# Values turned by VectorE and DRAM, position tables as one stationary square, and q two items ahead

## The reference, cut to what matters

```python
qkv = hidden_states @ qkv_w + qkv_b                      # 16 heads of 64
q, k, v = (qkv[0], qkv[1], qkv[2])
attn = jnp.einsum('bqc,bkc->bqk', q * scale, k)
rel_h = jnp.einsum('bhwc,hkc->bhwk', rq, Rh)             # rq: q by rows and columns
rel_w = jnp.einsum('bhwc,wkc->bhwk', rq, Rw)             # Rh[h, k] = rel_pos_h[h - k + 15]
attn = attn + rel_h[:, :, :, :, None] + rel_w[:, :, :, None, :]
attn = jax.nn.softmax(attn.reshape(B * nH, H * W, H * W), axis=-1)
out = attn @ v
return out @ proj_w + proj_b
```

## Time and profile before

| | us |
|---|---|
| median of 3 runs | 1245.13 (1244.61 to 1247.14) |
| the execution profiled | 1246.36 |
| its span | 1244.4 |
| TensorE busy | 1216.4 |
| VectorE / ScalarE / GpSimd busy | 690.4 / 475.1 / 641.5 |
| TensorE's mean granted clock, share of 2.4 GHz | 0.997 |

### The profile page before, as it was taken

The page is one execution under the profiler, slowest core; times in us unless marked ns, Lnnn a source line. Parts: engine busy times, 40 slices in busy tenths (PEclk is TensorE's granted clock), DMA queues, the critical chain, the costliest instruction groups (busy, mean ns, idle before and its releaser), DMA issues.

```text
span 1244.4 us, 19555 instructions
## 1 busy us (share of the span) xinstructions
PE 1216.4 (98%) x6768; PEld 975.0 (78%) x6768; DVE 690.4 (55%) x1434; ACT 475.1 (38%) x1229; POOL 641.5 (52%) x726
## 2 busy tenths in 40 slices
PE   6999999999999999999999999999999999889998
PEld 4788896478888888888888878777887787668887
DVE  7534444775665433666452578756347776476212
ACT  3611141034645320656341164644206555243212
POOL 4633389256565567555546655555665556464000
PEclk9999999999999999999999999999999999999999
DMA  5211124025564643454645356557535565620012
GB/s 185 84 46 48 34 56 117 8 65 160 154 169 137 184 134 97 127 177 128 185 136 166 86 160 212 180 160 223 168 102 151 175 209 156 205 60 1 29 40 68
DMA packets 129376, 155.03 MB, mean 125 GB/s; under 512 B 30080, under 2 KB 84000, under 8 KB 129280
## 3 DMA queue, kind: packets, MB, share of 16 engines
q1 hardware_dynamic: 118976, 146.92, 39.7%
q10 hardware_dynamic: 10304, 6.88, 1.8%
HBM read 111.81 MB, written 37.75 MB: 120 GB/s over the span
## 4 chain that ended last, share of the span: by engine, by line
PE 89%; DVE 5%; ACT 2%; issue 1%; DMA 1%; SPq 1%; POOL 0%; ACTq 0%; DVEq 0%; POOLq 0%
PE PS L1137 53%; PE PS L682 7%; PE PS L1758 7%; PE PS L1183 4%; PE PS L960 3%; PE PS L969 2%; PE PS L975 2%; PE PS L1227 2%; PE PS L1216 2%; PE PS L1775 2%; PE PS L1247 2%; PE PS L665 1%; PE PS L1197 1%; DVE bst L257 1%; PE PS L700 1%
## 5 line engine op out<-in xcount | busy, mean ns | idle before, releaser
L1137 PE MATMUL PS<-XB,w_hi 128*128 128x512 f32 x1024 | 340.5, 397 | 1.2 <-POOL w_lo L228 1.2
L226 POOL CAST w_hi<-w_raw 128x512 fp32r<-128x512 f32 x195 | 124.2, 637 | 307.5 <-PE PS L1137 213.0
L228 POOL TENSOR_TENSOR w_lo<-w_raw,w_hi 128x512 fp32r<-128x512 f32 x195 | 256.1, 1313 | 15.6
L1137 PEld LDWEIGHTS PS<-XB,w_hi 128*128 128x128 f32 x1024 | 192.2, 188 | 47.1 <-issue 5.0
L1137 PE MATMUL PS<-XB,w_lo 128*128 128x512 f32 x512 | 200.2, 391 | 0.0
L1137 PE MATMUL PS<-XB,part 128*128 128x512 f32 x768 | 190.3, 394 | 0.0
L1137 PEld LDWEIGHTS PS<-XB,part 128*128 128x128 f32 x768 | 141.9, 188 | 32.2 <-issue 2.3
L1373 ACT ACTIVATE part<-PS,nmax 128x256 f32<-128x256 f32 (+1 forms) x256 | 112.2, 443 | 141.6 <-DVE nmax L1485 93.2
L1383 ACT ACTIVATE part<-part,prec 128x256 f32<-128x256 f32 (+1 forms) x256 | 105.8, 476 | 27.7 <-DVE prec L1500 27.7
L228 POOL TENSOR_TENSOR part<-part,part 128x512 fp32r<-128x512 f32 x85 | 111.5, 1312 | 6.8
L1137 PE MATMUL PS<-part,w_hi 128*128 128x512 f32 x344 | 112.9, 395 | 1.5 <-DVE part L1544 1.5
(11 more groups left out here) (136 smaller groups left out, 1884.0 us busy)
## 6 DMA issues: line engine op xcount, KB each, us to landing
w_raw<-in_w SPq DMA_DIRECT2D x187, 256.0 KB, 2.8
part<-in_w SPq DMA_DIRECT2D x85, 256.0 KB, 2.8
turned<-part SPq DMA_DIRECT2D x128, 128.0 KB, 2.9
part<-turned SPq DMA_DIRECT2D x32, 512.0 KB, 5.0
turned<-part SPq DMA_DIRECT2D x128, 96.0 KB, 2.5
part<-turned SPq DMA_DIRECT2D x32, 384.0 KB, 4.0
strips<-part ACTq DMA_DIRECT2D x16, 256.0 KB, 2.7
out_x<-xT SPq DMA_DIRECT2D x16, 256.0 KB, 2.1
```

The costliest lines, as they stand in the source:

```text
L226: pool.tensor_copy(hi, raw).then_inc(w_hi_done, 1)
L228: pool.tensor_tensor(lo, raw, hi.bitcast(F32), ALU.subtract).then_inc(w_ready, 1)
L1137: m = nc.tensor.matmul(PS[:, bank, :], wt[:, (c % 4) * P:(c % 4) * P + P], rhs(hl, c), start=c == k == 0, stop=c == CK - 1 and k == 2)
```

## The change

- Values: V's product is turned in 32 × 32 blocks by DVE straight from PSUM (`turn_values`), written to DRAM by four DMAs, read back by one, and put in order by ACT (`take_v`). TensorE's four transposes go. The values' bias is added later, to the heads' result (the probabilities of a row sum to one).
- Position products: both tables and both heads form one stationary square of 128 × 128, q is the moving operand of 512 columns: 3 matmuls an item for 24. DVE turns the result (`turn_relative`), four DMAs write it.
- Order: Q's product of i+2 stands right behind K's of i+1. relative(i+2) stands in V's product of i after five chunks; attend(i−1) behind V's product (with j = 0 ahead of it). On ACT and DVE evac_q(i+2) and rest_of_q(i+2) stand near the end of item i, behind the normalization; evac_o(i−2) and rest_of_o(i−2) come first.
- Probabilities of all four head and image parts lie in one buffer and go to DRAM in four DMAs an item instead of eight.
- End: six PSUM banks for the last output product instead of three, its first halves spread over both last attends, and another placing of `build_m`.

The diff, cut to its core:

```diff
+            if i + 2 < ITEMS:
+                take_block(i + 2, "Q")
             take_block(i, "V", range(0 if i else 1, 2))
             if s and j == 0:
                 for o in range(CK):
                     take((s - 1, "O", o), STAGES[s - 1][0], "O", o)
-            if i + 2 < ITEMS:
-                take_block(i + 2, "Q")
...
         def relative(i):
-            for tt in range(4):
-                for k, (x, y) in enumerate(((qh[i % 2], rel_hi), (qh[i % 2], rel_lo), (ql[i % 2], rel_hi))):
-                    for hh in range(2):
...
+            pe.wait_ge(q_hi, i + 1)
+            pe.wait_ge(q_lo, i + 1)
+            for k, (x, y) in enumerate(((rel_hi, qh[i % 2]), (rel_lo, qh[i % 2]), (rel_hi, ql[i % 2]))):
+                m = nc.tensor.matmul(PS[:, X, :], x.rearrange("p r n -> p (r n)"), y.rearrange("p (a y x) -> p y a x", a=2, y=SIDE),
+                                     start=k == 0, stop=k == 2)
+            m.then_inc(rel_done, 1)
...
+        def values_block(i):
+            project(i, "V", range(0, 5))
+            relative(i + 2)
+            project(i, "V", range(5, CK))
...
         for i in range(1, LAST - 1):
             score_block(i)
             project(i + 1, "K", range(CK))
-            attend(i - 1, 0)
-            attend(i - 1, 1)
-            project(i, "V", range(CK))
...
+            project(i + 2, "Q", range(CK))
+            if i % PAIRS:
+                values_block(i)
+                attend(i - 1, 0)
+                attend(i - 1, 1)
+            else:
+                attend(i - 1, 0)
+                attend(i - 1, 1)
+                values_block(i)
...
     def attention_act(act):
+        def take_v(i):
+            act.wait_ge(v_in, 16 * (i + 1))
+            if i:
+                act.wait_ge(o_done, 2 * i)
+            dst = v.rearrange("p t (b c) -> p t b c", b=4)
+            nc.scalar.activation(dst, vB.rearrange("p (b t c) -> p t b c", b=4, t=4), ACT.Copy).then_inc(v_ready, 1)
...
-            if i:
-                evac_q(i + 1)
+            if i >= 2 and j != 1:
+                evac_o(i - 2)
             exps(i, 0)
...
             evac_k(i + 1)
+            if 0 < i < LAST:
+                take_v(i - 1)
             if 1 <= j <= 4:
                 for c in (2 * j - 2, 2 * j - 1):
                     norm.y(nc.scalar, s + 1, c)
                 for c in (2 * j - 2, 2 * j - 1):
                     norm.head(s + 1, c)
+            evac_q(i + 2)
+            if i and j == 0:
+                evac_o(i - 1)
+            if LO_KEYS <= i + 2 < ITEMS:
+                strips_to_dram(act, i + 2)
...
     def attention_dve(dve):
+        def turn_values(i):
+            product_done(dve, (i, "V"))
+            src = PS[:, bank_of(i, "V"), :].rearrange("p (t q c) -> p t q c", t=4, q=4)
+            dst = vB.rearrange("p (q t c) -> p t q c", q=4, t=4)
+            nc.vector.transpose(dst, src).then_inc(v_turned, 1)
...
-            if i:
-                rest_of_q(i + 1)
-            sum_relative(i, 0)
-            sum_relative(i, 1)
+            if i >= 2 and j != 1:
+                rest_of_o(i - 2)
             maxima(i, 0)
...
             if i < LAST:
                 rest_of_k(i + 1)
+            if j == 1:
+                norm.coefficients(s + 1)
+            if 1 <= j <= 4:
+                for c in (2 * j - 2, 2 * j - 1):
+                    norm.y(nc.vector, s + 1, c)
+                for c in (2 * j - 2, 2 * j - 1):
+                    norm.rest(s + 1, c)
+            rest_of_q(i + 2)
+            if i and j == 0:
+                rest_of_o(i - 1)
+            sum_relative(i + 1, 0)
+            sum_relative(i + 1, 1)
+            turn_relative(i + 2)
+            if i < LAST:
+                turn_values(i)
...
+    def values_to_dram(sp, i):
+        sp.wait_ge(v_turned, i + 1)
+        for b in range(4):
+            to = bass.AP(values.tensor, (i % 2) * P * 4 * P + P * b, [[4 * P, 32], [32 * 4 * P, 4], [1, P]])
+            sp.dma_start(to, vB[32 * b:32 * b + 32, :].rearrange("p (q r) -> p q r", q=4)).then_inc(v_out, 16)
+
+    def values_from_dram(sp, i):
+        sp.wait_ge(v_out, 64 * (i + 1))
+        sp.dma_start(vB, values[i % 2, :, :]).then_inc(v_in, 16)
```

More of the change, by code:

```diff
@@ L1106, in later_layers @@
     S, PT, O, X = 2, 4, 6, 7
-    REL = (X, 0)
     LO_KEYS = 2 * PAIRS
@@ L1455, in attention_act @@
                     norm.head(s + 1, c)
+            evac_q(i + 2)
[3 more added lines that the diff above has]
+                strips_to_dram(act, i + 2)
+        evac_o(LAST - 1)
+        take_v(LAST)
         evac_o(LAST)
@@ L1581, in attention_dve @@
             turn_probs(i, 2)
-            if i and j == 0:
-                rest_of_o(i - 1)
+            if i == LAST:
+                turn_values(i)
             invert_sums(i, 3)
@@ L1599, in attention_dve @@
                 norm.group_stats(s + 1)
-            if j or i == 0:
-                take_v(i)
-            if j == 0:
-                norm.coefficients(s + 1)
-            if 1 <= j <= 4:
-                for c in (2 * j - 2, 2 * j - 1):
-                    norm.y(nc.vector, s + 1, c)
-                for c in (2 * j - 2, 2 * j - 1):
-                    norm.rest(s + 1, c)
+        rest_of_o(LAST - 1)
         rest_of_o(LAST)
         for o in range(CK):
-            for k in M_AFTER.get((o, 0), ()):
-                rest_of_m(dve, k)
+            if o >= 6:
+                for k in M_AFTER[o, 0]:
+                    rest_of_m(dve, k)
+                for k in (2 * o - 12, 2 * o - 11):
+                    stats_of(3, k)
             add_out(3, o)
-            if o:
-                stats_of(3, o - 1)
             for k in M_AFTER[o, 1]:
                 rest_of_m(dve, k)
-        stats_of(3, CK - 1)
+        for o in range(4, CK):
+            stats_of(3, o)
         norm.aggregate(5, range(CK), 16)
@@ L1651, in probs_from_dram @@
+            sp.dma_start(to, row[:, :, at:at + w]).then_inc(p_out[a or 0], 16)
     def probs_from_dram(sp, i, a):
-        w = 8 * squares(i) * 32
-        sp.wait_ge(p_out[a], 64 * (i + 1))
+        run = 2 * squares(i) * 32
+        if i == LAST and a:
+            sp.wait_ge(p_out[1], 64)
+        else:
+            sp.wait_ge(p_out[0], 64 * (i + 1))
         if i:
             sp.wait_ge(o_done, 2 * i - 1 + a)
-        sp.dma_start(probT[:, a, 0:w], turned[i % 2, a, :, 0:w]).then_inc(p_in[a], 16)
```

256 lines of the change are left out of this document (114 added, 142 removed).

## The result

The changed kernel takes 1266.22 us (median of 4 runs, 1265.87 to 1268.13), the kernel before beside it 1245.59 (1244.61 to 1247.14): 1.0175 times the time, 95% interval 1.0162 to 1.0187. It is 20.6 us slower where the forecast said 11. The profiled spans are 1264.7 and 1244.4 us.

A forecast was written before the change was run, and what follows sets the result against it. TensorE was taken to bound the kernel (busy 1216.4 of 1244.4 us). Savings −41.4, q waits +21.6 and +15.0, j = 0 +3.6, ties +0.5, clock +12 sum to +11.3: 1256 us, range 1238 to 1270.

The forecast's parts named there:

- What TensorE loses: TensorE work saved by transposes, tables, fewer array switches and a shorter end: −41.4 us in sum.
- steps a to c: TensorE savings: four value transposes per item −14.1 us, table matmuls 24 to 3 −13.3, one array-use switch less −3.
- step (c): Attend directly ahead of the next scores saves one whole-array to part-array change per item: −3 us (0 to −8).
- The cover for the values' way and for the weights: Values' DRAM path ready about 15 us after next scores, needed at 18; weights don't lack issue time: no cost.
- The q chain: Relative waits for q_lo in layer 2: 3.6 us in j = 2 to 4 (+21.6), 7.5 in j = 1 (+15.0).
- The clock: TensorE's clock falls to half after nearly each of the eight q waits: 8 × 1.5 = +12 us (0 to 16).
- The end, step (d): From scores of item 30 to the last layer, six PSUM banks and new order save 11 us (4 to 12.4).
- j = 0: Attend(i−1) ahead of the values waits 1.8 us for take_v(i−1), twice: +3.6 us (2 to 6).
- Rival 3: ACT's four strips DMA issues in normalizing items delay evac_o and the maxima: slower yet, 1276 us; chance 13%.
- Rivals 1 and 2: First: waits stay but clock holds (1244 us) or rests are short too (1236), 18%; second: see Rival 2.
- Rival 2: q_lo in time if within 14.5 us of the maxima: 1208 us, or 1227 at half the waits; chance 13%.

The follow-up runs named there:

- the last kernel: Changed kernel with q's evacuation and rest ahead of norms, values' copy early in items j = 0 and 30, ACT's strips issues behind next item's evac_o: 1214.66 us.
- the fill experiment: Changed kernel plus unused dummy matmuls ahead of relative in the eight waiting items, 13 each, 24 in j = 1: 1253.68 us.
- q first: Changed kernel with q's evacuation and rest moved ahead of take_v and the norms on ACT and DVE: 1236.87 us.
- experiment 2: Changed kernel with the four DMAs of the position sums' strips issued by SP instead of ACT: 1267.49 us.
- qfirst_sp: Changed kernel with q's evacuation and rest ahead of take_v and the norms, and the strips' DMAs issued by SP: 1233.76 us.
- the last two kernels: Changed kernel with q ahead of norms and values' copy early (items j = 0, 30): 1226.56 us; then strips issues also moved behind next item's evac_o: 1214.66 us.
- experiment 4: Changed kernel with ACT's copy of the values inside the softmax, behind normalize(i, 2), in every item: 1256.05 us.

## Why the prediction was right, and where it was not

**What TensorE loses: right.** The item of layer 1 fell by 0.76 us; 0.54 was said. The three table matmuls cost little over their 512 columns (0.80 us, said 0.68): in the last kernel an item of layer 2 without a wait lasts 20.8 us, 1.5 less than before, where steps a to c said 1.4 (22.28 − 0.44 − 0.83 − 0.1 = 20.9). Start to item 17 came out 2.7 us better than said, so step (c)'s 3 us was low; whether it is the switch of array use alone was not measured apart. The cover for the values' way and for the weights held as well: in items 17 to 23 and 25 to 29 no attend waits for the copy, and TensorE's waits at weights are 1.4 us in all.

**The q chain: right in its place and its size.** Maxima at 1.51 (1.5 said), relative at 19.56 (19.6 said), a wait of 3.37 (3.6) in each of six items. In j = 1 relative came at 22.2 instead of 23.5 and waited 5.99 instead of 7.5: the two rests took 1.29 us there, not 2.56. DVE's record of the same instruction differs by a factor of two from item to item, as the earlier trace rows showed; I had taken the one of item 19 for both.

**The clock: right in kind, too small.** All eight items fell to half clock, and the fill experiment prices that at 16.3 us against 12. I had counted one stretch of 3.41 us for each fall, as rows 5 have it; five of the eight lasted 6.83. The two errors, waits 4.4 us shorter and clock 4.3 dearer, cancel, which is luck. The Trainium skill (TensorE: Matmul & The Clock Gate, "HAM oscillation — how this bites in real kernels") advises, for a loop of thin matmuls that waits for a DMA in each turn, to restructure the loop so that TensorE keeps its clock. Here the order of q's evacuation did that: with q first two of the eight falls are left (items 17 and 25), in the last kernel one (item 17).

**The end, step (d): the step that failed.** It promised 11 us and walked only to attend(31); from item 30 on, 13.5 us were to be gained and 6.3 were, so that (d) brought some 4 us instead of 11. Up to the last output block the end takes 83.4 us, where 78 was said. Behind the scores of item 31 it came true: TensorE's waits fall from 8.4 us to 2.0, and the 3.4 us of lost clock there go but for 0.9 that item 30 leaves behind. (The landing of 5.0 us in rows 6, which it took as the most, is a median; attend(31) did not wait for one.) But in item 30 there is no Q block any more, so attend(29) comes at t0 + 12.8 and needs take_v(29), which ACT does behind the whole softmax. That is the very mechanism I priced for j = 0, with the same arrival, and did not look for in item 30. ACT's issues of item 29 add to it: evac_o starts 2.0 us after the scores of item 30, the maxima at 3.35. Its timeline, and the stretch behind the wait:

```profile
1066.60 1.70 PE L1179 MATMUL PS<-part,part 64*128 64x256 f32 x24
1082.24 0.61 ACT L1340 ACTIVATE part<-part 128x512 f32<-128x512 f32 x1
1082.95 3.68 PE L1200 MATMUL PS<-part,part 128*64 128x256 f32 x16 [3.55 <-issue]
```

```profile
1083.00:1088.00 5.00, 5.00 (x28) 3.27 (x30) 2.57 (x5) 0.69 (x1) 0.00 (x0) 0.50 0.94 271
```

The 3.55 us of wait and 2.6 of clock are 6.2 of the 7.2 by which the end missed: 6.8 us are at half clock, of which 1.5 lie inside the wait. Behind the scores of item 31 the four waits of `build_m` cost 2.0 us, where the forecast left 1.4 for all waits. With the strips on SP (experiment 2) item 30 has the copy where it was and no issues ahead of evac_o:

```profile
1084.38 1.95 PE L1200 MATMUL PS<-part,part 128*64 128x256 f32 x16 [2.22 <-issue]
```

So 2.2 us of the wait are the copy's place and the other 1.3 the issues'. The clock held behind the shorter wait in this run; with q first besides (qfirst_sp) it fell for 3.4 us behind the same 2.2. In the last two kernels, where the copy is early, item 30 lasts 15.5 us. Even there not all of it comes back: from item 30 to the end they take 196.6 and 194.6 us, against 198.1 in the changed kernel and the 190.9 of the forecast, since with a shorter item 30 TensorE waits 0.9 and 0.8 us for K's rest ahead of the scores of item 31 and 1.9 and 1.5 us at attend(31), in the first of them with 1.7 us of clock behind it.

**j = 0: too small.** Attend in items 16 and 24 waited 2.81 and 3.55 us, not 1.8. In item 24 the maxima start at 3.2 instead of 1.5, since evac_o stands behind ACT's issues, which I had set to zero.

**Rival 3: right mechanism, wrong items.** I put ACT's issues into the normalizing items. There the long wait gave them room (maxima at 1.5 in items 18 to 20); they bit in items 16, 22, 23, 24 and 30, where no wait for q stood ahead of them. They are most of what was missed outside the end: items 21 to 24 came out 3.4 us worse than said. When the q wait was removed they became the next bound, in nearly every item of layer 2.

**Rivals 1 and 2** did not happen. Rival 2's condition, q_lo ready within 14.5 us of the maxima, is true already with q first (relative starts 13.8 to 14.0 us behind late maxima there), and that kernel runs at 1236.9, not 1208: the maxima slipped instead, as in rival 3. Only with the issues moved as well, 1214.7 us, does the time come near rival 2's.

## What to carry over

When work is moved earlier in one engine's program, its inputs on the other engines must move too: list for every consumer what stands ahead of its producer, and do it again in each item whose order differs, first and last ones above all. Price a wait of some 3 us or more on TensorE with what the clock then takes, here 2 us on average for each of the eight. And a DMA issue is work of the engine that issues it: put it where that engine waits anyway, and do not count another queue as free without its timeline.

## What the runs showed of the chip that I had not expected

- The issue of a DMA costs ACT's time: the four strips issues of 64 KB took 0.56 to 1.6 us each (median 0.65), where the one of 256 KB before took 0.37.
- Waits at relative of 3.37 us and more were followed in all eight items by half clock. Shorter waits went either way: in the last kernel two of 2.5 us kept full clock and one of the same length (item 17) did not, of six of 3.2 us (experiment 4) one kept it, and of two of 2.2 us in item 30 one. What decides between them the runs don't show.
- The same DVE instruction on the same shape, the norm's rest, took from 0.68 to 1.68 us in the changed kernel. Which other access it shares time with was not tried apart.
- The tables' product, with its moving operand read in runs of 16 positions, cost hardly more than plain ones: at full clock 0.80 us from its first matmul to the next block's, 0.68 by the earlier trace rows. Item 21 of the changed kernel:

```profile
819.54 0.96 PE L1227 MATMUL PS<-part,part 128*128 128x512 f32 x3 [0.18 <-issue]
820.34 0.39 PE L1137 MATMUL PS<-XB,w_hi 128*128 128x512 f32 x1
```
